# A fused gated-delta-rule and expert layer: six chunks per loop iteration, the block inverse merged by VectorE, sums of squares taken from transposed tiles

## What is computed

```python
def attn(x):                                     # x: layernormed tokens
    mixed = silu(causal_conv4(x @ Wqkv.T + bqkv))   # q, k: 8 heads of 128, v: 16 heads of 128
    q, k, v = split(mixed); q, k = l2norm(q) * 128 ** -0.5, l2norm(k)   # repeated to 16 heads
    beta, g = sigmoid(x @ Wb.T + bb), -exp(A_log) * softplus(x @ Wa.T + ba + dt_bias)
    for t in tokens:                             # a state of 128 x 128 for each head
        S = S * exp(g_t)
        S = S + k_t outer ((v_t - k_t @ S) * beta_t)
        out_t = q_t @ S
    out = out * rsqrt(mean(out ** 2) + eps) * norm_w * silu(x @ Wz.T + bz)
    return out @ Wout.T + bout
x = x + layernorm(attn(layernorm(x)))
x = x + layernorm(experts(layernorm(x)))         # a shared expert and 16 routed ones, 8 of 16 weighted per token
```

## Time and profile before

| | before |
|---|---|
| median of 3 runs (lowest to highest) | 3548.47 us (3543.68 to 3554.87) |
| the profiled execution: time, span | 3551.05 us, 3549.2 us |
| TensorE busy (weight loads) | 3291.3 us, 93% (2920.5 us) |
| VectorE, ScalarE, GpSimd busy | 2714.1 us (76%), 2423.9 us (68%), 2145.0 us (60%) |
| mean granted clock of TensorE | 0.963 |
| DMA | 143.89 MB, mean 41 GB/s |

### The profile page before, as it was taken

The page is one execution under the profiler, slowest core; times in us unless marked ns, Lnnn a source line. Parts: engine busy times, 40 slices in busy tenths (PEclk is TensorE's granted clock), DMA queues, the critical chain, the costliest instruction groups (busy, mean ns, idle before and its releaser), DMA issues.

```text
span 3549.2 us, 86916 instructions
## 1 busy us (share of the span) xinstructions
PE 3291.3 (93%) x23968; PEld 2920.5 (82%) x24096; DVE 2714.1 (76%) x8720; ACT 2423.9 (68%) x5922; POOL 2145.0 (60%) x5380
## 2 busy tenths in 40 slices
PE   4999999999999999999999999999999999999986
PEld 4888888888888888888888888888888888888875
DVE  4777777877777777778787777777778777778773
ACT  3777667767767766777776777676677676677662
POOL 3766666666656656666666666666666666566660
PEclk8999999999999999999999999999999999999996
DMA  4111111111111111111111111111111111111110
GB/s 173 42 37 40 41 34 39 38 36 36 41 37 33 41 39 36 35 42 35 36 45 36 34 42 35 36 42 39 34 42 35 36 37 44 35 35 43 36 41 4
DMA packets 424188, 143.89 MB, mean 41 GB/s; under 512 B 211168, under 2 KB 421664, under 8 KB 423200
## 3 DMA queue, kind: packets, MB, share of 16 engines
q1 hardware_dynamic: 423712, 139.83, 15.1%
HBM read 93.11 MB, written 46.66 MB: 39 GB/s over the span
## 4 chain that ended last, share of the span: by engine, by line
PE 71%; ACT 13%; issue 8%; DVE 4%; POOL 2%; DMA 2%; DVEq 0%; SPq 0%; ACTq 0%; POOLq 0%
PE bF L464 9%; PE bB L635 6%; PE bQ L545 5%; PE bXT L553 4%; ACT L809 4%; PE bF L475 3%; PE bB L691 3%; PE bS L602 3%; PE bF L477 3%; PE bB L685 3%; PE bD L617 3%; PE bS L610 3%; PE bS L594 3%; PE bX L558 2%; PE bD L595 2%
## 5 line engine op out<-in xcount | busy, mean ns | idle before, releaser
L1103 DVE SCALAR_TENSOR_TENSOR Y<-bF,Cv,Y 128x127 f32<-128x127 f32 (+2 forms) x3072 | 852.0, 339 | 33.9 <-ACT Y L826 29.0
L464 PE MATMUL bF<-XnT,Wqkv 128*128 128x128 f32 x4096 | 556.5, 286 | 0.5 <-ACT XnT L945 0.5
L464 PEld LDWEIGHTS bF<-XnT,Wqkv 128*128 128x128 f32 x4096 | 530.1, 202 | 9.5 <-issue 2.1
L826 ACT ACTIVATE Y<-bF,Cv 128x128 f32<-128x128 f32 x1024 | 387.7, 456 | 151.4 <-PE bF L464 107.4
L896 ACT ACTIVATE XiT<-bXT 128x512 fp32r<-128x512 f32 x384 | 228.7, 596 | 296.2 <-PE bXT L553 295.1
L1531 POOL TENSOR_TENSOR Tp<-Tp 32x64 f32<-32x64 f32 (+2 forms) x768 | 361.3, 470 | 60.2
L1146 DVE TENSOR_TENSOR Qi<-bQ,Cf 128x512 fp32r<-128x512 f32 x384 | 264.0, 687 | 97.6 <-PE bQ L545 96.4
L809 ACT ACT_TABLE_LOAD x257 | 329.7, 1283 | 5.4 <-PEq L1615 0.7
L553 PE MATMUL bXT<-Qi,Xi 128*128 128x128 f32 x1536 | 301.9, 319 | 2.4 <-DVE Qi L1146 2.4
L553 PEld LDWEIGHTS bXT<-Qi,Xi 128*128 128x128 f32 x1536 | 222.1, 192 | 96.2 <-DVE Qi L1146 47.3
L1524 POOL TENSOR_TENSOR Tp<-Yb,Tm 32x64 f32<-32x64 f32 (+1 forms) x384 | 276.9, 721 | 30.1
(11 more groups left out here) (198 smaller groups left out, 9272.2 us busy)
## 6 DMA issues: line engine op xcount, KB each, us to landing
DL<-Ln SPq DMA_DIRECT2D x128, 256.0 KB, 2.2
XiT<-DX SPq DMA_DIRECT2D x128, 256.0 KB, 2.8
Xi<-DX SPq DMA_DIRECT2D x128, 256.0 KB, 3.2
DX<-Yb SPq DMA_DIRECT2D x256, 32.0 KB, 1.8
Xf<-x SPq DMA_DIRECT2D x32, 128.0 KB, 3.2
Wqkv<-wqkv SPq DMA_DIRECT2D x4, 1024.0 KB, 17.1
Cb<-DL SPq DMA_DIRECT2D x128, 32.0 KB, 1.9
Xr<-x SPq DMA_DIRECT2D x32, 128.0 KB, 2.9
```

What stands on the lines that cost most here:

```text
L464: last = mm(bank[:, i, :], Wqkv[:, k, c:c + P], XnT[:, k, :], start=(k == 0), stop=(k == KT - 1))
L826: last = op(Y[:, tile, :], bank[:, i, :], ACT.Identity, scale=c[:, TAPS - 1:TAPS], bias=c[:, TAPS:TAPS + 1])
L1103: last = stt(y, bank[:, i, 0:P - shift], Cv[:, g * TILES + tile, n:n + 1], y, ALU.mult, ALU.add)
```

## The change

It has four parts, made together.

1. The loop over the 30 middle chunks holds six chunks in its body and runs five times. The instructions of a chunk stay the same.
2. `invert_begin` is gone. The first level's products are written to bXT and bX alone (not added to anything), and VectorE adds them to XiT and Xi in SBUF (`merged_t`, `merged`). At the second and third level ScalarE copies only the new blocks out of PSUM (`new_blocks`). At the third level the products read 64 rows and write 64 columns of each head, and VectorE's mask is a copy of 64 partitions.
3. `ss` is gone. `ktr` transposes all four tiles, queries and keys, as soon as silu is done. ScalarE squares each of the four from PSUM with the sum over the row written out (`accum_out` into Ssq), and VectorE reads these.
4. The orders of TensorE, ScalarE and VectorE are new. GpSimd's and SyncE's stay. Two experts' jobs move to the next item: D0 from g = 1 to the head of g = 2, D2 from g = 2 to the head of g = 3. U0 moves on VectorE from g = 1 to g = 2.

```diff
-            with eng.Fori(1, chunks - 1) as t:
-                for g in range(GROUPS):
-                    item((t, g), "cafispe")
+            steps = next(n for n in (6, 5, 3, 2, 1) if (chunks - 2) % n == 0)
+            with eng.Fori(0, (chunks - 2) // steps) as i:
+                for k in range(steps):
+                    for g in range(GROUPS):
+                        item((i * steps + k + 1, g), "cafispe")
...
-            def ss(f):
...
             def ktr(f):
                 t, g = f
-                pe.wait_ge(sem["sse_done"], at("sse_done", f))
-                for kh in range(GK):
-                    last = nc.tensor.transpose(heads(bXT)[:, kh, :], QK[:, g, 2 * kh + 1, :], ident)
+                pe.wait_ge(sem["xt_done"], at("xt_done", ahead(f, -2)))
+                pe.wait_ge(sem["silu_done"], at("silu_done", f, 1))
+                for i in range(2 * GK):
+                    last = nc.tensor.transpose(heads(bXT)[:, i, :], QK[:, g, i, :], ident)
...
-                mm(bXT[:, :], IdR[:, 0, :], XiT[:, :, :], start=True, stop=True)
-                mm(bX[:, :], IdR[:, 0, :], Xi[:, :, :], start=True, stop=True)
+            def halves(n):
+                if n < LEVELS - 1:
+                    return (slice(0, P),) * 3
+                return slice(0, P // 2), slice(P // 2, P), slice(0, P // 2)
+
+            def invert_q(v, n, front=None):
                 if n == 0:
+                    if front:
+                        pe.wait_ge(sem["ex_done"], at("ex_done", ahead(v, 1)))
...
+                    last = mm(heads(bQ)[:, h, left], LnR[upper, h, :], XiT[upper, h, left], start=True, stop=True)
...
+                    last = mm(heads(bXT)[:, h, left], Xi[lower, h, :], Qi[lower, h, left], start=True, stop=True)
...
             def square_qk(f):
+                act.wait_ge(sem["ktr_full"], at("ktr_full", f))
+                act.wait_ge(sem["sse_done"], at("sse_done", ahead(f, -1)))
+                for i in range(2 * GK):
+                    last = op(Sq[:, i, :], heads(bXT)[:, i, :], ACT.Square, accum_out=Ssq[:, i:i + 1])
+                last.then_inc(sem["sq_done"], 1)
...
+            def new_blocks(bank, buf, n, below):
+                b = BASE << n
+                for o in range(0, P, 2 * b):
+                    rows, cols = slice(o + b, o + 2 * b), slice(o, o + b)
+                    if not below:
+                        rows, cols = cols, rows
+                    last = op(buf[rows, :, cols], heads(bank)[rows, :, cols], ACT.Copy)
+                return last
...
+                if l == LEVELS - 1:
+                    rows, cols = slice(P // 2, P), slice(0, P // 2)
+                    nc.vector.tensor_copy(Qi[rows, :, cols], heads(bQ)[rows, :, cols]).then_inc(sem["q_done"], 1)
...
+            def merged_t(v):
+                dve.wait_ge(sem["xt_full"], at("xt_full", v, 1))
+                tt(XiT[:, :, :], heads(bXT), XiT[:, :, :].bitcast(F32), ALU.add).then_inc(sem["xt_done"], 1)
+
+            def merged(v):
+                dve.wait_ge(sem["x_full"], at("x_full", v, 1))
+                tt(Xi[:, :, :], heads(bX), Xi[:, :, :].bitcast(F32), ALU.add).then_inc(sem["xi_done"], 1)
```

More of the change, by code:

```diff
@@ L543, in invert_q, with invert_xt @@
                     pe.wait_ge(sem["q_done"], at("q_done", v, n))
+                upper, lower, left = halves(n)
                 for h in range(GH):
-                    last = mm(heads(bQ)[:, h, :], LnR[:, h, :], XiT[:, h, :], start=True, stop=True)
+                    last = mm(heads(bQ)[:, h, left], LnR[upper, h, :], XiT[upper, h, left], start=True, stop=True)
                 last.then_inc(sem["q_full"], 1)
-            def invert_xt(v, n):
+            def invert_xt(v, n, front=None):
+                if n == 0 and front:
+                    pe.wait_ge(sem["partsT_done"], at("partsT_done", ahead(v, 1)))
+                elif n == 0:
+                    pe.wait_ge(sem["xt_done"], at("xt_done", ahead(v, -1)))
                 pe.wait_ge(sem["q_done"], at("q_done", v, n + 1))
@@ L731, in item @@
                     exponents(f)
-                if state:
-                    az(w, 0)
-                    new_state(w, 0)
-                if new:
-                    proj(a, 1, 1)
-                if e and g == 1:
-                    experts(t - 1, "hT", 0)
-                if invert:
-                    invert_begin(v, front)
-                    invert_q(v, 0)
                 if c and g == 1:
@@ L755, in item @@
                 if invert:
-                    invert_q(v, 1)
+                    invert_q(v, 0, front)
+                if e and g == 1:
+                    experts(t - 1, "ffn1", 0)
+                if state:
+                    ks_qs(w, 1)
+                if invert:
+                    invert_xt(v, 0, front)
+                    invert_x(v, 0, front)
                 if state:
                     solve(w, 1)
+                if invert:
+                    invert_q(v, 1)
                 if post:
@@ L762, in item @@
                     invert_xt(v, 1)
-                    invert_x(v, 1)
-                if e and g == 2:
-                    experts(t - 1, "D", 1)
                 if state:
@@ L768, in item @@
                 if invert:
+                    invert_x(v, 1)
                     invert_q(v, 2)
+                if e and g == 2:
+                    experts(t - 1, "D", 1)
                 if e and g == 1:
@@ L989, in item @@
                 if front:
+                    key_norm(f)
                     keys(f)
@@ L992, in item @@
                     query_state(w, 0)
+                if post:
+                    core_t(u)
+                if state:
                     solved(w, 0)
+                if new:
+                    last_tap(a, 1)
                 if front:
@@ L996, in item @@
                     scales(f)
-                if post:
-                    core_t(u)
+                if e and g == 1:
+                    experts(t - 1, "hT", 0)
                 if front:
@@ L1026, in item @@
                     experts(t - 1, "norm1", 0)
-                if e and g == 2:
-                    experts(t - 1, "G", 2)
+                if front:
+                    rounded_l(f)
                 if e and g == 1:
@@ L1322, in item @@
                     right_side(w, 0)
+                if e and g == 1:
+                    experts(t - 1, "hn", 0)
+                if e and g == 2:
+                    experts(t - 1, "U", 0)
+                if new:
+                    ended(a)
+                if post:
+                    gated(u)
+                if c and g == 1:
+                    chunk_front(t + 1, "sp")
                 if e and g == 2:
                     experts(t - 1, "D", 0)
+                if e and g == 3:
+                    experts(t - 1, "D", 2)
@@ L1325, in item @@
                 if front:
                     squares(f)
-                if new:
-                    ended(a)
                 if state:
                     refined(w)
-                if post:
-                    gated(u)
+                if new:
+                    taps(a, 0, 2)
                 if front:
                     products(f)
-                if c and g == 1:
-                    chunk_front(t + 1, "sp")
                 if new:
-                    taps(a, 0, 2)
                     taps(a, 0, 1)
-                if e and g == 1:
-                    experts(t - 1, "hn", 0)
+                    taps(a, 0, 0)
```

225 lines of the change are left out of this document (103 added, 122 removed).

## The result

| | us, median (runs) | ratio to before | profiled span | clock |
|---|---|---|---|---|
| before | 3548.28 (13), 3543.68 to 3555.07 | 1 | 3549.2 | 0.963 |
| changed | 3561.68 (13), 3555.84 to 3570.89 | 1.0042 [1.0031, 1.0052] | 3559.1 | 0.984 |

Slower by 0.42%. The forecast was 3352, so 210 us are missing.

A forecast was written before the change was run, and what follows sets the result against it. The prediction took TensorE's matmuls to bound three items of four. From the profiled 3551 us, turns -115, TensorE's relief -146 and new waits +64 gave 3354, or 3352 against the median; range 3300 to 3400, at 50%.

The forecast's parts named there:

- Turns: Loop's jumps: 25 fewer at 4.6 us each, -115 us; fetching straight ahead taken as 0.
- TensorE's relief, -146: TensorE, every item: identity products and ss products out, two transposes more, 1.14 us an item, 128 items, -146 us.
- the 150 to 250 that I gave as a sign: Sign that the forecast is right: TensorE's busy time lower by 150 to 250 us.
- VectorE's +0.94 us: VectorE, every item: two merges +1.22, last mask as a smaller copy -0.28; net +0.94 us busy.
- the forecast's rule: VectorE's copy at partition 64: output in another quadrant waits for earlier instructions; 0.07 us each for it and its follower.
- ScalarE: Head of ScalarE's item: four squares take 1.3 us in all, busy time hardly changes, Ex ends at 11 to 11.5.
- The waits, +0.5 us an item: New order: TensorE's head waiting for Ex, and VectorE late; 0 to 1.5 us an item, taken as 0.5, +64 us.
- The last level by halves at 0: Inverse's last level on TensorE: same eight matmuls with half the rows and columns, weight loads stay, 0 us.
- (b): Rival: latency from Ex through transfers and base inverse to the next item replaces TensorE; 3431 to 3480; 26% with (d).
- (c): Rival: slower, ScalarE's squares at the item's head over 0.7 us each delay Ex and TensorE; 3623 at 0.85; 5%.
- (d): Rival: the turns' price stays because other engines' code stalls in the long body; -115 missing, 3467; 26% with (b).
- (a): Rival: TensorE stays the bound without new waits; 3290, down to 3250 with the upper price of a turn; 16%.

The follow-up runs named there:

- six chunks alone: The kernel before with only the loop changed, six chunks in the body and five iterations: 3420.76 us, ratio 0.9645.
- the kernel with Ex early: Old-order kernel with six chunks, transposed squares and three moves (3505.32), with ScalarE's decays and TensorE's exponents moved forward: 3541.79 us, ratio 0.9974 to before.
- the first run: The run six chunks alone, the kernel before with only the loop body lengthened: 3420.76 us, ratio 0.9645.

## Why the prediction was wrong

*Turns: right.* -115 forecast, 102 to 126 measured. Straight code costs nothing that can be seen: q8 went from 19 packets in all to 206 and 211 (six chunks alone), and in that kernel the items g = 1 to 3 take 27.65, 25.99 and 24.57 us, within 0.1 of the earlier trace rows. At the four turns that are left TensorE now idles with nothing that the profile shows, for 3.5, 1.8, 1.8 and 1.9 us, where before its wait there was for VectorE; the longest:

```profile
839.84 1.19 PE L598 MATMUL bS<-S,QK 128*128 128x256 f32 x2 [3.51 <-issue]
```

The Trainium skill (Runtime: NRT & Kernel Launch, Instruction fetch mechanics) has a stall for a taken branch out of the resident window; the row agrees.

*TensorE's relief, -146: this step failed.* The instructions did leave: in one chunk in mid-run the four ss groups (3.4 us) and the identity products (2.2) are gone. TensorE's busy time fell by 83 us, not by the 150 to 250 that I gave as a sign, and 66 of these already fall in six chunks alone. I wrote that as the items g = 1 to 3 leave TensorE almost no air, its relief is a gain of the time. But idle times of 0.05 to 0.8 us do not say that a shorter TensorE makes a shorter item: a ring of waits, in which one item waits over the other engines for the item before, can be nearly as long. Taken away alone in the old order the work gave 30 us. That is 116 of the 210 missing.

*VectorE's +0.94 us, which I hid under its 3.8 to 6.4 us of air: wrong in the other direction, in the old order.* The air was a mean over the item. The merges lie between two masks that follow each other, mask, product, merge, product, mask, where ScalarE's copies of XiT and Xi ran beside VectorE. Merging alone lengthens the tail by 1.7 us an item. In the new order the whole inverse costs 22 us against the old one, 17 of them for the halves. The copy at partition 64, which no row had shown, is held as the forecast's rule has it: the operation behind it starts 0.04 us after its end (1720.28 against 1720.24 in the changed kernel), where behind a full mask the next one starts 0.08 before the end (1726.68 against 1726.76).

*ScalarE: size about right, place underrated.* Four squares take 1.14 us from the first's start to the last's end (1728.79 to 1729.93) for 1.3 forecast; an ACTIVATE lasts 282 ns, its accumulator read 215, and they overlap. But their place is later. The old square does not end before the item begins, as I had it: over the 16 items of six chunks alone it ends 2.9 us after TensorE's start of the item and Lnk begins at 4.6. In the changed kernel the last square ends at 4.75 and Lnk begins at 6.5, since last_tap(0) now also stands between the sums and Lnk (0.7 of the 1.9 us; whether the changed kernel gains by moving it was not tested). Lnk releases GpSimd, the parts and Ex. In the changed kernel Ex ends at 12.0, not 11 to 11.5.

*The waits, +0.5 us an item: mis-sized.* The forecast comes to (107.28 - 4.6) / 4 - 1.14 + 0.5 = 25.0 us an item; it is 26.63. That is 1.6 too much, 205 us, and it is the whole miss: 0.9 is the relief that did not come (the 116 us above), and 0.7 an item is what the new waits cost beyond the 0.5 I allowed. This split supposes that the two add up, which no run shows. I had named two waits (Ex, Xi); the wait of kkq for the last mask, 1.1 us in the head shown, was not in my list, though the diff puts kkq second in the item and the mask last.

*The last level by halves at 0 (bounds -0.3 and +0.1 us an item):* it costs 17 us, 0.13 an item.

*Rivals.* (b), a ring over Ex, the transfers and the base inverse, exists: it is the chain of the kernel with Ex early. In the changed kernel itself GpSimd and the transfers have 1% each of the chain, so there it was not what held the time. And I let it cost only what Ex moved beyond its air, 3431 to 3480, and priced it as one ring; as I read the runs there are several, over VectorE's masks, ScalarE's seam and GpSimd, all nearly as long as TensorE's work. (c), the slower case, was priced with squares over 0.7 us each; they took 0.28 and the kernel is slower all the same. (d) fell with the first run. In (a), 3250 is a slip: with the upper price of a turn the sum gives 3240.

*The new order* is not the culprit as a whole: the edits cost 135 and 181 in the old order, which would make 3737 if they added up; with the new one they come to 3562: 119 for the squares and the order together, and 22 for the inverse. It shortens the tail (14.07 against 14.54) and pays in the head (12.56 against 10.97).

*What stays open:* whether an order exists in which these edits get under 3421. Nor was the new order run with neither edit, so the 119 us that remain without the new inverse are not divided between the squares and the order; moving last_tap(1) or kkq alone made the kernel slower.

## What to carry to other kernels

When the busiest engine idles under 1 us in an item, that does not show that it alone bounds; it can be level with a ring of waits: leave its work out in one run before you count its relief as time, as here 1.16 us an item left out gave 30 us of 148. Cover for added work is counted between the two instructions it stands between, not over the item; work moved from a parallel engine into the queue that makes the next mask was on the path at once in one order, and nearly free in another. And take the part of a change that has one mechanism by itself: longer straight bodies gave 3.6 to 3.9%, the rest took all of it away.

## What the runs showed of the hardware

Two instructions side by side in the changed kernel: a small VectorE operation of 128x32 whose two inputs both lie in SBUF (line 1256 reads Xba twice) lasts as long as GpSimd's 32x512 product that began 0.08 us before it; here the last mask, and kkq behind it, come after it.

```profile
1724.59 1.51 POOL L1553 TENSOR_TENSOR Tp<-Yb,Tm 32x512 f32<-32x512 f32 x1
```
```profile
1724.67 1.49 DVE L1256 SCALAR_TENSOR_TENSOR Ab<-Xba 128x32 f32<-128x32 f32 x1
1726.08 0.68 DVE L1161 TENSOR_TENSOR Qi<-bQ,Cf 128x512 fp32r<-128x512 f32 x1
```

They end 0.06 us apart. The Trainium skill (SBUF — State Buffer, Terms) has a port pair that VectorE and GpSimd share, and the loser blocks for the whole instruction; the rows agree. The same holds for 31 of the 32 times that it runs: it ends 0.05 to 0.06 us behind the GpSimd instruction that was under way, short or long. In the one case with none under way it takes 0.19 us. The kernel before has the same operation, but there it mostly meets shorter ones:

```profile
L1235 DVE SCALAR_TENSOR_TENSOR Ab<-Xba 128x32 f32<-128x32 f32 x32 | 11.1, 348 | 1.1
```
```profile
L1256 DVE SCALAR_TENSOR_TENSOR Ab<-Xba 128x32 f32<-128x32 f32 x32 | 37.6, 1176 | 1.1
```

That is 0.83 us more in each chunk, 26.5 in all, in front of a mask that TensorE waits for. How much of it the time pays no run shows by itself.

Products with half the rows and columns are no cheaper: four of 64x64 take 0.56 us from the first's start to the next group (1118.96 to 1119.52), four of 128x128 0.50 (1199.69 to 1200.19 in six chunks alone).
